# A layer norm moved from token tiles to feature tiles, with the last block, the dense weights and the row loads in another order

## The reference

```python
    x = x + _L0_conv_ref(_ln_c(x), ...)
    t = _to_tokens(x)
    t = t + _L0_ffn_ref(_ln_t(t), L0_ffn_gate_w, L0_ffn_gate_b, L0_ffn_w1, L0_ffn_w2, L0_ffn_w3)
    x = _from_tokens(t, x)
...
    def _ln_t(v, eps=1e-05):
        m = jnp.mean(v, axis=-1, keepdims=True)
        s = jnp.var(v, axis=-1, keepdims=True)
        return (v - m) / jnp.sqrt(s + eps)
...
        logits = jnp.einsum('bsd,de->bse', x, gate_w) + gate_b
        probs = jax.nn.softmax(logits, axis=-1)
        top_probs, top_idx = jax.lax.top_k(probs, 2)
        top_probs = top_probs / jnp.sum(top_probs, axis=-1, keepdims=True)
        dispatch = jnp.sum(jax.nn.one_hot(top_idx, n_experts, dtype=x.dtype) * top_probs[..., None], axis=-2)
        h1 = jnp.einsum('bsd,edh->bseh', x, w1)
        h2 = jnp.einsum('bsd,edh->bseh', x, w2)
        hidden = jax.nn.silu(h1) * h2
        expert_out = jnp.einsum('bseh,eho->bseo', hidden, w3)
        return jnp.einsum('bseo,bse->bso', expert_out, dispatch)
```

## Time and profile before

| | |
|---|---|
| median of 3 runs | 1144.78 us |
| the profiled execution | 1150.03 us, its span 1148.2 us |
| mean granted TensorE clock | 0.954 |
| PE busy | 972.6 us (85%) |
| DVE busy | 873.9 us (76%) |
| ACT busy | 763.8 us (67%) |
| POOL busy | 369.1 us (32%) |
| block 23 up to the row numbers of batch 0 | about 919 to 966 us |
| dense part of batch 0 on PE | 966.5 to 1014 us |
| units 0 to 9 | 1014.7 to 1055.2 us |
| units 10 to 19 | 1067.5 to 1105.9 us |
| dense part of batch 1, last sums, stores | 1106.4 to 1148.2 us |

### The profile page before, as it was taken

The page is one execution under the profiler, slowest core; times in us unless marked ns, Lnnn a source line. Parts: engine busy times, 40 slices in busy tenths (PEclk is TensorE's granted clock), DMA queues, the critical chain, the costliest instruction groups (busy, mean ns, idle before and its releaser), DMA issues. The chain is left out here.

```text
span 1148.2 us, 47596 instructions
## 1 busy us (share of the span) xinstructions
PE 972.6 (85%) x20326; PEld 573.8 (50%) x20326; DVE 873.9 (76%) x1372; ACT 763.8 (67%) x1486; POOL 369.1 (32%) x410
## 2 busy tenths in 40 slices
PE   4889888988899898888989898888899876877797
PEld 2455444554455454545545454544555443456664
DVE  5789877987789788777988789777988787652255
ACT  3777777787778876787778777776887652322122
POOL 8522131321322312223223231232232213634725
PEclk9899999999999999999999999999999986879789
DMA  3411110201011001011011110101110021335621
GB/s 74 143 43 32 33 32 16 47 9 31 16 32 42 16 16 25 27 33 37 10 25 33 32 36 3 32 20 31 39 36 14 15 68 33 102 79 146 154 66 40
DMA packets 113226, 49.31 MB, mean 43 GB/s; under 512 B 85688, under 2 KB 106488, under 8 KB 113016
## 3 DMA queue, kind: packets, MB, share of 16 engines
q1 hardware_dynamic: 99544, 40.49, 13.8%
q0 software_dynamic: 3072, 3.15, 1.1%
q10 hardware_dynamic: 10400, 2.62, 1.0%
HBM read 23.62 MB, written 9.44 MB: 29 GB/s over the span
## 5 line engine op out<-in xcount | busy, mean ns | idle before, releaser
L1743 DVE TENSOR_TENSOR em<-em,gs 128x1536 f32<-128x1536 f32 (+1 forms) x192 | 300.3, 1583 | 10.1 <-ACT em L1360 9.5
L1360 ACT ACTIVATE em<-ring 128x512 f32<-128x512 f32 x480 | 248.8, 598 | 25.6 <-PE ring L1025 21.1
L1045 PE MATMUL ybank<-em,xdt 64*32 64x64 f32 (+1 forms) x12288 | 181.7, 238 | 32.6 <-issue 30.0
L1045 PEld LDWEIGHTS ybank<-em,xdt 64*32 64x32 f32 x12288 | 151.6, 106 | 94.9 <-issue 63.3
L571 POOL TENSOR_TENSOR ysq<-yg 128x512 f32<-128x512 f32 x96 | 109.1, 1136 | 278.4 <-DVE yg L1763 274.7
L1025 PE MATMUL ring<-rt,lt 128*64 128x512 bf16 x960 | 148.3, 398 | 21.0 <-ACT em L1360 12.1
L578 POOL TENSOR_TENSOR x_t<-on,x_b 128x256 f32<-128x256 f32 x48 | 41.8, 871 | 202.0 <-DVE on L1771 202.0
L1771 DVE TENSOR_TENSOR on<-oss,rr 128x256 f32<-128x256 f32 x96 | 40.4, 421 | 81.8 <-ACT rr L1370 76.9
L1750 DVE SCALAR_TENSOR_TENSOR yt<-xs,col,ybank 128x256 f32<-128x256 f32 x192 | 82.9, 472 | 23.7 <-PE ybank L1045 23.5
L1025 PEld LDWEIGHTS ring<-rt,lt 128*64 128x64 bf16 x960 | 45.1, 110 | 107.3 <-issue 42.4
L578 POOL TENSOR_TENSOR x_b<-on,x_b 128x256 f32<-128x256 f32 x48 | 35.0, 730 | 195.3 <-DVE on L1771 195.3
(11 more groups left out here) (266 smaller groups left out, 1839.0 us busy)
## 6 DMA issues: line engine op xcount, KB each, us to landing
rt<-wcat SPq DMA_DIRECT2D x80, 96.0 KB, 1.9
x_b<-x_t SPq DMA_DIRECT2D x48, 128.0 KB
cm<-bc SPq DMA_DIRECT2D x24, 224.0 KB, 2.7
rt<-lt SPq DMA_DIRECT2D x120, 24.0 KB
sorted_y<-yt ACTq DMA_DIRECT2D x10, 256.0 KB, 3.1
sorted_x<-h_b SPq DMA_DIRECT2D x4, 512.0 KB, 4.4
cw<-in_L_conv_t_cw SPq DMA_DIRECT2D x6, 320.0 KB
cw<-in_L_conv_b_cw SPq DMA_DIRECT2D x6, 320.0 KB
```

The source lines that it names most:

```text
L1045: mm = pe.matmul(ybank[QUAD * q:QUAD * (q + 1), ab, to:to + hi - lo], xdt[m % 2][rows, 8 * (i % 2) + 4 * first + q, r, :], em[rows, p % EM ...
L1360: emptied(act.activation(em[:, p % EM_SLOTS, :, HALF * j:HALF * (j + 1)], o.rearrange("p (h t) -> p h t", h=HEADS), ACT.Exp), "seg", n, i, ...
L1743: dve.tensor_tensor(e, e, gs[n % 2][:, i:i + 1, 0:wide].to_broadcast([P, HEADS, wide]), ALU.mult).then_inc(s_w, 1)
```

## The change

The norm is computed where the features lie on the partitions (`normed` runs on POOL, `deviation` and `variance` on PE, `square_of` and `root_of` on ACT). PE makes the deviation from the mean straight from `x_t` and the centred input (a new constant `off_mean`, identity minus mean, and four turns accumulated in the same bank), ACT squares and copies it, PE averages the squares, ACT takes logarithm and exponential, POOL multiplies. Only the normed rows are turned to tokens, for the scatter. The input's mean, which the in-place `center` now takes out of `x_in`, is added back between the units (`add_means`).

```diff
+            const(pool.tensor_tensor(out=off_mean[:], in0=ident[:], in1=mean64[:], op=ALU.subtract))
...
+            def normed(q):
...
+                pool.tensor_tensor(out=x2[:, cols], in0=x2[:, cols], in1=dsq[q % 2], op=ALU.mult).then_inc(s_xn, 1)
...
+            def deviation(q, o):
+                pe.wait_ge(s_x, 4 * LAST + (0, 0, 2, 4)[q])
+                pe.matmul(o, off_mean[:], x_t[:, CK * q:CK * (q + 1)], start=True, stop=False, skip_group_check=True)
+                for j in range(4):
+                    mm = pe.matmul(o[:, P * j:P * (j + 1)], x_in[:, 4 * q + j, :, :].rearrange("p b c -> p (b c)"),
+                                   ident[:], start=False, stop=True, skip_group_check=True)
...
+            def variance(q, o):
+                pe.wait_ge(s_d2, q + 1)
+                return pe.matmul(o, mean64[:], dsq[q % 2], start=True, stop=True)
...
+            def square_of(q, o):
...
+                act.activation(dsq[q % 2], o, ACT.Square).then_inc(s_d2, 1)
...
+                return act.activation(x2[:, CK * q:CK * (q + 1)], o, ACT.Copy)
...
+            def root_of(q):
+                act.activation(dsq[q % 2], dsq[q % 2], ACT.Exp, scale=-0.5).then_inc(s_rs, 1)
```

Block 23 leaves the loops (`for k in range(LAST)`) and is written out by hand on PE, ACT, DVE and POOL. The ends of the hand-written order, first on ACT, then on DVE:

```diff
+            inverse_root(LAST, 3)
+            selectors(0)
+            selectors(1)
+            early_square(2)
+            first_rows()
+            last_square()
+            early_root(2)
+            last_root()
             exp_second(0)
...
+            norm_out(LAST, 2)
+            norm_out(LAST, 3)
+            first_logits()
             largest()
-            norm_out(LAST, 2)
             second_largest()
-            norm_out(LAST, 3)
```

In the dense part of batch 0 the norm of batch 1 goes, and the picks, row numbers and owners of batch 1 come early; the four quarters of `x_t` are turned back and added to `x_in` there (`back`, `add_back`):

```diff
             places(0, filled("rank", LAST, 0))
+            owners(0)
             weigh_x(0)
...
                 if k == 0:
-                    owners(0)
+                    second_logits()
                 dense_hidden(k)
                 if k == 1:
-                    second_sum(0)
-                    second_sum(1)
+                    largest()
                 if k == 2:
-                    center(3)
+                    second_largest()
+                if k == 3:
+                    join_picks()
                 if k == 4:
-                    sum_squares(3)
...
+                    dve.wait_ge(s_rank, 1)
+                    places(1, oss)
+                    owners(1)
+                if k in (8, 10, 12, 14):
+                    add_back((k - 8) // 2)
...
             units(0)
+            for b in range(NBATCH):
+                add_means(b)
             units(1)
+            share_picks(1)
+            weigh_picks(1)
+            split_mix()
```

SP copies w1 and w2 once, during block 1, into DRAM in row order, so that the dense weights are later loaded in runs of 4 KB, and its last part has another order; the scatter waits for the copied rows, the row loads for the turns back:

```diff
+                sp.dma_start(w1d, a["w1"].rearrange("e c h -> c e h")).then_inc(s_cat, 16)
+                sp.dma_start(w2d, a["w2"].rearrange("e c h -> c e h")).then_inc(s_cat, 16)
...
-                        sp.dma_start(w1s[hi][rows], a["w1"][es].rearrange("e c h -> c e h")).then_inc(s_ew, 16)
+                        sp.dma_start(w1s[hi][rows], w1d[:, es, :]).then_inc(s_ew, 16)
...
                 sp.wait_ge(s_sc[b], 16 * 2 * NSP)
+                sp.wait_ge(s_bt2, 2 * (b + 1))
...
-            unit_weights(0, 0, UNITS // 2)
+            unit_weights(0, 0, 7)
             sp.wait_ge(s_x, 4 * NBLOCK)
             unit_x(0)
-            unit_weights(0, UNITS // 2, UNITS)
+            unit_weights(0, 7, UNITS)
             sp.wait_ge(s_owner, 2)
-            unit_weights(1, 0, UNITS // 2)
-            sp.wait_ge(s_x1, 2)
+            unit_weights(1, 0, 3)
             unit_x(1)
-            unit_weights(1, UNITS // 2, UNITS)
+            unit_weights(1, 3, UNITS)
...
                 pool.wait_ge(s_place, b + 1)
+                pool.wait_ge(s_rows, 2 * (b + 1))
```

More of the change, by code:

```diff
@@ L127, in ring_turns @@
     t.one("mean", 1, 0)
-    for k in range(NBLOCK):
+    for k in range(LAST):
         n = k + 1
@@ L131, in ring_turns @@
         t.seg(k, 3)
-        if k == LAST:
-            t.two("back", k)
         t.seg(k, 4)
@@ L151, in ring_turns @@
         t.seg(n, 1)
-    t.two("feat", LAST)
+    t.seg(LAST, 2)
+    t.seg(LAST, 3)
+    t.seg(LAST, 4)
+    t.one("cent", LAST, 0)
+    t.seg(LAST, 5)
+    t.one("var", LAST, 0)
+    t.seg(LAST, 6)
+    t.seg(LAST, 7)
+    t.one("cent", LAST, 1)
+    t.one("var", LAST, 1)
     t.one("gate", LAST)
+    t.one("cent", LAST, 2)
+    t.one("rows", LAST, 0)
+    t.one("rows", LAST, 1)
+    t.one("var", LAST, 2)
     t.one("rank", LAST)
@@ L180, in build @@
         mean64 = sb("mean64", [P, P])
+        off_mean = sb("off_mean", [P, P])
         ones64 = sb("ones64", [P, HALF])
@@ L579, in add_x @@
                                    op=ALU.add).then_inc(s_x, 1)
-            for k in range(NBLOCK):
+            def normed(q):
+                pool.wait_ge(s_rs, q + 1)
+                if q == 3:
+                    pool.wait_ge(s_dc, 1)
+                else:
+                    c, count = turn["cent", LAST, q]
+                    pool.wait_ge(s_read[c], count + 1)
+                cols = slice(CK * q, CK * (q + 1))
+                pool.tensor_tensor(out=x2[:, cols], in0=x2[:, cols], in1=dsq[q % 2], op=ALU.mult).then_inc(s_xn, 1)
+            for k in range(LAST):
                 if k:
@@ L851, in first_gate, with first_rows @@
                 pe.wait_ge(s_gw, 16 * 4)
-                for half in range(2):
-                    read("feat", LAST, 0, half)
+                pe.wait_ge(s_xn, 2)
                 filled(gate(0, take("gate", LAST, 0)), "gate", LAST, 0)
+            def first_rows():
+                for q in range(2):
+                    filled(four_turned(take("rows", LAST, q), x2, 4 * q), "rows", LAST, q)
             def ranks(b, o):
@@ L1199, in dense @@
                 spread_mix(first + 2)
+                if d == 0:
+                    second_gate()
                 for k in range(first + 1, last, 2):
@@ L1439, in copy_gram, with early_square, early_root, last_square @@
                     act.nop().then_inc(s_gram, 1)
-            def first_x2():
-                for half in range(2):
-                    o = filled("feat", LAST, 0, half)
-                    emptied(act.activation(x2[:, CK * half:CK * (half + 1)], o, ACT.Copy), "feat", LAST, 0, half)
+            def square_of(q, o):
+                if q >= 2:
+                    act.wait_ge(s_xn, q - 1)
+                act.activation(dsq[q % 2], o, ACT.Square).then_inc(s_d2, 1)
+                if q == 0:
+                    act.wait_ge(s_yg, 4 * LAST)
+                    act.wait_ge(s_xt, 4 * LAST)
+                return act.activation(x2[:, CK * q:CK * (q + 1)], o, ACT.Copy)
+            def early_square(q):
+                emptied(square_of(q, filled("cent", LAST, q)), "cent", LAST, q)
+            def root_of(q):
+                act.activation(dsq[q % 2], dsq[q % 2], ACT.Exp, scale=-0.5).then_inc(s_rs, 1)
+            def early_root(q):
+                o = filled("var", LAST, q)
+                emptied(act.activation(dsq[q % 2], o, ACT.Ln, bias=eps5[:]), "var", LAST, q)
+                c, count = turn["var", LAST, q]
+                act.wait_ge(s_read[c], count + 1)
+                root_of(q)
+            def last_square():
+                act.wait_ge(s_tp, NCK + 1)
+                square_of(3, bank[6]).then_inc(s_dc, 1)
+            def last_root():
+                act.wait_ge(s_gt, 1)
+                act.activation(dsq[1], oss[:], ACT.Ln, bias=eps5[:]).then_inc(s_vl, 1)
+                act.wait_ge(s_vl, 1)
+                root_of(3)
+            def rows_to(q, o):
+                return act.activation(sq[:, CK * q:CK * (q + 1)], o, ACT.Copy)
+            def first_rows():
+                for q in range(2):
+                    o = filled("rows", LAST, q)
+                    emptied(rows_to(q, o), "rows", LAST, q)
+                    c, count = turn["rows", LAST, q]
+                    act.wait_ge(s_read[c], count + 1)
+                    act.nop().then_inc(s_rows, 1)
+            def second_rows(half):
+                act.wait_ge(s_tp, NCK + 2 + half)
+                rows_to(2 + half, oss[:]).then_inc(s_rows, 1)
             def selectors(half):
```

259 lines of the change are left out of this document (146 added, 113 removed).

## The result

The changed kernel takes 1128.32 us (median of 4 runs, 1126.28 to 1131.39) against 1145.35 (1143.15 to 1146.44) beside it: ratio 0.9847, 95% interval 0.9819 to 0.9875. Forecast were 1123, a range of 1111 to 1135 and a gain of 21.7; the gain is 17.0 by the medians and 20.1 by the spans of the two profiles (1148.2 and 1128.1). Timed again later it was 1127.25 (ratio 0.9833, 0.9806 to 0.9860).

A forecast was written before the change was run, and what follows sets the result against it. DVE's list bounds block 23's end, PE the dense part, late row loads behind weights the units. -7.5 + 1.8 - 6.8 - 9.9 + 0.7 = -21.7 from 1150.03 gives 1128.3; less 5.25, 1123 (own range 1117 to 1129; with rivals 1111 to 1135).

The forecast's parts named there:

- B: Dense part of batch 0: more turns on PE and changed waits, 50.0 us against 48.2, +1.8.
- A: Block 23 up to the row numbers of batch 0: less DVE work, some waits kept, end at 958.6 against 966.13, -7.5.
- POOL and DVE: Within block 23: POOL's four new products slow DVE at one meeting, 0.7 us; 4.9 by the skill page's rule.
- C1: First turned rows to end of first `expert_out`: row numbers no longer there, PE clock stays up, 8.0 us against 14.8, -6.8.
- C2: First to last `expert_out`: earlier row loads of batch 1, SP's issuing sets the pace, 66.4 us against 76.3, -9.9.
- D: Tail: `split_mix` of batch 1 behind the last unit on DVE, partly hidden, +0.7; +2.2 if nothing hides it.
- At nothing: Copies to DRAM, POOL's `off_mean` and dense-weight loads priced at zero; uncovered, copy issues 2.5 us and `off_mean` 0.3.
- The base: Whole kernel: sum taken from the profiled 1150.03, then lowered 5.25 because the runs' median was 1144.78.
- first rival: Only the queue helps: PE's clock stays at half through the dense part, -13.4, 1131 us; chance 15%.
- the second: Rival: waits close up in the dense part and SP issues without hiccups, -31.6, 1113 us; chance 13%.
- the third: Rival: row loads of batch 1 come no earlier and the 12.26 us wait stays, -11.8, 1133 us; chance 4%.
- The fourth: Rival: PE idles in each unit and its clock falls to half, 4.87 us a unit, slower at 1161 us; chance 4%.

The follow-up runs named there:

- experiment 3: Changed kernel with the shares' exponential of batch 0 earlier on ACT: 1125.56 us; with ranks and the gate of batch 1 also earlier on PE: 1122.09 us.
- experiment 4: Changed kernel with DVE's row numbers of batch 1 cut into two pieces, behind experts 4 and 5: 1126.74 us.
- experiment 1: Changed kernel with SP's old grouping of weight and row loads: 1135.31 us; kernel before with the new grouping alone: 1139.30 us.
- experiment 2: Changed kernel with sorted-row loads issued by POOL instead of SP: both batches 1149.99 us, batch 1 alone 1127.55 us.
- experiment 7: Changed kernel with earlier exponential, ranks and gate, split row numbers, batch 1 rows loaded by POOL, and batch 1 mix made amid the units: 1115.26 us.
- experiment 5: Changed kernel with dense weights read from the inputs: 1131.95 us with the row-order copies still made, 1129.74 us without them.
- early exponential: Changed kernel with only the shares' exponential of batch 0 moved ahead on ACT, right behind the square of quarter 2: 1125.56 us.

## Why the prediction was right or wrong

Against the profiled execution the sum said 1128.3, and it was 1129.85. That this miss is so small is partly luck: behind it stand a term that was too good by 4.5 us and, the other way, the 1.5 us ahead of the first mark and a B that came out 1.0 shorter than forecast.

- **A is the step that failed.** Forecast was the end of the row numbers at 958.6, 40.15 us behind the first weighing; it came at 961.57, 44.63 behind it. The work was right: 31.57 us with POOL's price in it, against 31.3 and 0.7. The waits were not. They were put at 7.6 us (4.0 for the last quarter, 2.0 gate, 1.6 exponential); the trace has 2.8 for the roots, 1.8 for the gate, 3.7 for the exponential, and 2.9 for inputs of weighings and products, which the forecast put at nothing: 11.2, and 1.3 more in small gaps between steps. So the two terms that failed are the exponential, too small by 2.1, and the unpriced inputs. Of these the longest, 1.81, is for an exponential of ACT (L1449). The shares' exponential could be had earlier: experiment 3, which only moved it in ACT's list, takes 2.2 to 2.4 us off A. The forecast counted ACT's operations ahead of it, but not that ACT itself would stand 3.64 us for PE's deviation at a lower clock; at full clock DVE's wait is 2.27.
- **POOL and DVE.** Priced at one meeting of 0.7. Two of the four products fall in DVE's waits, as said; the others cost some 0.4 (DVE's product of 0.69 us took 1.07) and 1.0 us. By the rule of the Trainium skill, page "SBUF — State Buffer", section "SBUF: two separate sides", the loser is blocked for the whole instruction of the other: the trace agrees, since DVE's step ends at 955.51, just behind POOL's product at 955.47, and the two steps of experiment 3 end at 955.18 and 956.34 beside products that end at 954.90 and 956.30. The 4.9 us by that rule needed all four products to meet DVE's work, which they do not.
- **B, right.** 49.0 and 47.8 against 50.0, in the first 43.93 us of work and 5.3 of waits against 44.4 and 5.6. The waits were forecast as a size only. Experiments 3 and 4 show what the new order gave away: the gate amid the dense part (clock 0.50 from 964 to 968) and the row numbers in one piece, 3 to 4 us each by stage.
- **C1, right:** 8.2 against 8.0, in every run of the new order but the one whose rows came late (13.0). The 4.21 us became 0.89, and the clock stayed at 1.00. The place of the row numbers is the reason argued; that it is not the queue, experiment 1 shows. No run undoes the new norm and keeps the new place of the row numbers, so their shares in A, B and C1 are not separated.
- **C2, right in size, half right in reason:** 66.1 and 66.4 against 66.4. Experiment 1 shows the regrouping to be nearly all of it (10.1 us undone, 9.3 alone). But SP does not set it alone: PE waited for weights once, and experiment 2 took 3.4 us off C2 by moving three small loads, though not off the time.
- **D:** 42.9 and 44.8 against 43.1; the change's two profiles part in the clock of the first 8 us behind the last product, 0.79 and 0.57:

```profile
1085.16:1093.16 8.00, 5.42 (x28) 3.11 (x29) 5.31 (x17) 2.08 (x6) 3.33 (x4) 0.79 0.26 59
1083.52:1091.52 8.00, 6.28 (x26) 3.28 (x25) 4.99 (x16) 2.08 (x6) 3.33 (x4) 0.57 0.25 59
```

  The mix was on the path, as PE's wait there shows, and experiment 7 took it off:

```profile
PE ring L931 <- DVE gs L2022: 1.3, 1, 1.3
```

- **At nothing:** in doubt for the dense weights (experiment 5). The copies and the constant do not show: without the copies the first mark lies at 915.88, amid the others.
- **The base.** The remaining 3.7 of the 5.3 us between 1123 and 1128.32: the profiled execution of the kernel before lay 5.25 above the runs' median, and that was taken off the sum; the change's two lie 1.5 and 2.8 above theirs.
- **Rivals.** By the number alone 1128.32 lies nearer to the first rival's 1131 than to 1123; the stages decide. The first (only the queue helps) is refuted by C1 and by the units' start at 1010.84, the second (the waits close up) by B and C2, the third (rows late) by the 2.04 us; experiment 2's miss shows what late rows cost. The fourth, units at half clock, appears in small: behind the wait of 2.04 us the mean clock from 1045 to 1060 is 0.77, and in the early exponential's profile it is 0.50 at the end, where a last product takes 1.91 us instead of 1.10 and C2 some 4 us more. The Trainium skill, page "TensorE: Matmul & The Clock Gate", section "HAM oscillation — how this bites in real kernels", describes a loop in which the wait for DMA ahead of each piece of work puts the clock back for that piece. Here single waits did so; no run shows it going on from unit to unit through the batches.

## What to carry to other kernels

In an in-order DMA queue, put a small load that is soon needed ahead of large ones that must wait for buffers: that regrouping, four lines, gave some 7 of the 17 us of this change. When a step is moved to the end of an engine's list, price its wait by everything ahead of it, the waits of that engine and a lower clock of whoever feeds it included. And make the sum against the profiled execution, but do not carry that execution's excess over the median into the forecast.

## What the runs showed that was not expected

The same code gave the row numbers 42.8 to 46.1 us behind the same mark, in six profiles. DVE's steps agree to 0.3 us for the first 25 us; the first to differ are the logits, which wait for PE's gate product, and the later end goes with a lower granted clock of PE from 28 to 38 us behind the mark (1.00, four of 0.83 to 0.87, 0.74). A step of DVE on 16 columns took 1.16 us for 0.17 beside a POOL product. And a chain of short PE products with waits between them costs up to 3 us more or less from one execution to the next, which is as much as most of the single edits here.
